# Attention passes of a graph network: the weights of a group move from SBUF into PSUM, behind the scan's multipliers

## The chip, the cores and the metric

One Trainium2 chip, one of its cores. The metric is the device time of one execution in microseconds. The kernel before was run three times: median 13124.66 us, 13120.15 to 13129.22 us.

## What is computed

Four graph layers follow one another over 12500 nodes and 200000 edges sorted by target node, each behind a layer norm and added to its input. The change touches the attention of the second and third layer. For every edge a score is made per head, a softmax runs over the edges of one target node, and the weighted rows of the source nodes are summed:

```python
e = alpha_s[src] + alpha_d[dst]
e = jnp.where(e > 0, e, NEG_SLOPE * e)
m = jax.ops.segment_max(e, dst, num_segments=num_nodes)
w = jnp.exp(e - m[dst])
denom = jax.ops.segment_sum(w, dst, num_segments=num_nodes)
alpha = w / (denom[dst] + 1e-16)
out = jax.ops.segment_sum(alpha[:, :, None] * h[src], dst, num_segments=num_nodes)
```

This attention runs three times with 4 heads of 16 features: once in the second layer (there the score has an edge term too) and twice in the third.

## The kernel before

Each of the 128 partitions owns 1563 consecutive edges. A pass (`gat_edges`, L2070) walks over them in 98 groups of 16 edge columns; the last two groups are cut into four smaller pieces. The rows of the source nodes land in a ring `y` of six groups (an iteration of the loops is these six). Of the 96 columns of an iteration three sources fetch:

- GpSimd (POOL) gathers 86 by indirect DMA, one instruction a column (L2129; 1403 in a pass). It waits only for the ring's slot to be free, by the signal `weighted` (L2126).
- SyncE (SP) fetches two, row by row with 128 small DMAs each (`SyncRows`, L338; its DMAs are L333), after the same signal.
- TensorE fetches eight out of a table in SBUF by matmuls with a unit matrix (`ColumnFetch`, L382; the matmuls are L475). VectorE adds up what they give (L483) and picks the half that is wanted (L511, L514); these are the "points" in VectorE's step.

VectorE then does one `step` for each group: scores (L2195 to L2204), running maximum by scans (L2210), differences (L2222 to L2226), then, once ScalarE has written the weights `ex` = exp(s - max) (L2285): a copy of `ex` into the scan's input (L2232), the weighting of the rows, a multiply of 1024 elements a partition, `y` by `ex` into `w_in` (L2233, which raises `weighted`), and the scan that carries the softmax sum along the edges with the multipliers `r` = exp(old max - new max) (L2240, which raises `summed`). ScalarE's part of a group, in its order: exp for `ex`, exp for `r` (L2290, 1088 elements), the load of the next edge attributes (L2305, second layer's pass alone), the load of TensorE's places (L451, L456), and the finished rows `row` out to memory (L2298 to L2302). The `r` lies in three banks of PSUM of which it uses 1156 of 1536 words; `ex` lies in SBUF.

The order around the change is set by each engine's own program order and by these semaphores:

```python
act.wait_ge(*shifted(pc.n + 1))
...
act.activation(ex[:, :, 0:w], de[:, 1, :, 0:w], ACT.Exp).then_inc(exps.h, 1)
act.wait_ge(*summed(pc.n))
...
v.wait_ge(*weighted[b](i + 1))
v.wait_ge(*r_ready(g + 1))
```

`summed(pc.n)` is the scan of the group before, which VectorE has done before it raises `shifted`. The passes of the first layer (`conv_edges`, L1012) are built alike, with one head of 97 features; their gathers are L1059, their weighting is L1118 (1552 elements), and their `ex` lies in PSUM, in a bank of its own.

Of the kernel before, what the change touches and what calls it, by code (L numbers as in the profile page):

```python
# [25 lines left out]
P = 128  # L26
# [4 lines left out]
GW = 16  # L31
# [74 lines left out]
def piece(i, b):  # L106

    return Piece(i * 2 + b, i, b, b, i, 0, GW, (i * 2 + b) * GW, GW)
# [51 lines left out]
def narrow(t, w):  # L160

    flat = t.rearrange("p f t -> p (f t)")
    return flat[:, 0:flat.shape[1] // (GW + 1) * (w + 1)].rearrange("p (f t) -> p f t", t=w + 1)
# [90 lines left out]
def build(nc, a, out):  # L254
# [13 lines left out]
    h = table[:, NCOL // 2:].rearrange("p (c f) -> p c f", f=D)  # L268
# [37 lines left out]
    def by_edge(t):  # L306
        return t[0:EP, :].rearrange("(p t) f -> p t f", p=P)
# [1762 lines left out]
    def gat_edges(tag, rows, bd=None):  # L2070

        H, J1 = HG, JG + 1
        F = H * J1
        st = Stage(nc, tag, signals)
        y = st.sb("y", [P, NY, GW, TG])
        ad_raw, ad = st.sb("ad_raw", [P, ET, H]), st.sb("ad", [P, H, ET])
        s0, s, fm = st.sb("s0", [P, H, GW]), st.sb("s", [P, H, GW]), st.sb("fm", [P, 2, H, GW + 1])
        de, ex, ex_bank = st.sb("de", [P, 2, H, GW]), st.sb("ex", [P, H, GW]), st.ps("z0", [P, 512])
        r_banks, w_in = st.ps("r", [P, 1536]), st.sb("w_in", [P, H, J1, GW + 1])
        r_flat = r_banks[:, 0:F * (GW + 1)].rearrange("p (f t) -> p f t", f=F)  # L2080
        r, w_flat = (r_banks[:, 0:F * (GW + 1)].rearrange("p (h j t) -> p h j t", h=H, j=J1),
# [15 lines left out]
            eadded = st.sem("eadded", NPIECE)  # L2097
        taken = SYNC_SLOTS + [c.slot for c in FETCHED]
        gathered, by_sync = st.pass_slots(taken), SyncRows(st, y, g_tab, TG, 1)
        other_bank = [] if bd is not None else [st.ps("z1", [P, 512])[:, 0:2 * TG]]  # L2100
        fetch = ColumnFetch(st, (pa, pb), [ex_bank[:, 0:2 * TG]] + other_bank,
                            row[:].rearrange("p b t f -> p (b t f)")[:, 0:1024].rearrange("p (b f) -> p b f", b=2),
# [3 lines left out]
        weighted, row_ready, den_in = (st.piece_slots(n) for n in ("weighted", "row_ready", "den_in"))  # L2106
# [3 lines left out]
        exps, r_ready, summed = (st.sem(n, NPIECE) for n in ("exps", "r_ready", "summed"))  # L2110
# [3 lines left out]
        with nc.Block(no_gpsimd_drain=True) as block:  # L2114
            @block.sync
            def _(sp):
                sp.wait_ge(*signals["scattered0"](0))
                sp.dma_start(ad_raw[:], by_edge(ad_start)).then_inc(ad_loaded.h, 16)
                by_sync.all_columns(sp, weighted)
# [156 lines left out]
            @block.scalar  # L2276
            def _(act):
                def weights(pc):
                    w = pc.w
                    act.wait_ge(*shifted(pc.n + 1))  # L2280
                    if pc.b == 1:
                        act.wait_ge(*weighted[0](pc.i + 1))
                    else:
                        act.wait_ge(*weighted[1](pc.i))
                    act.activation(ex[:, :, 0:w], de[:, 1, :, 0:w], ACT.Exp).then_inc(exps.h, 1)  # L2285
                    act.wait_ge(*summed(pc.n))
                    if w < GW:
                        act.activation(narrow(r_flat, w)[:, :, 0:1], same[:, 0:1].unsqueeze(1).to_broadcast([P, F, 1]),
                                       ACT.Copy, scale=0.0)
                    act.activation(narrow(r_flat, w).rearrange("p (h j) t -> p h j t", h=H)[:, :, :, 1:w + 1],  # L2290
                                   de[:, 0, :, 0:w].unsqueeze(2).to_broadcast([P, H, J1, w]), ACT.Exp)\
                        .then_inc(r_ready.h, 1)

                def send(pc):
                    b, w = pc.b, pc.w
                    act.wait_ge(*summed(pc.n + 1))
                    act.wait_ge(*row_stored[b](pc.i * 16))
                    act.activation(row[:, b, 0:w, F:F + H], fm[:, b, :, 1:w + 1].rearrange("p h t -> p t h"), ACT.Copy)  # L2298
                    act.activation(row[:, b, 0:w, 0:F], narrow(acc[:, b], w)[:, :, 1:w + 1].rearrange("p f t -> p t f"),  # L2299
                                   ACT.Copy).then_inc(row_ready[b].h, 1)  # L2300
                    act.wait_ge(*row_ready[b](pc.i + 1))
                    act.dma_start(by_edge(rows)[:, bass.ds(pc.col, w), :], row[:, b, 0:w]).then_inc(row_stored[b].h, 16)  # L2302

                def edge_attrs(i, b, w=GW):
                    act.dma_start(ea[0:8 * w, b, :], a["edge_attr_8"][bass.ds((i * 2 + b) * P, 8 * w), :])\  # L2305
                        .then_inc(e_loaded[b].h, 16)

                def group(n, j, more=True):
                    i, b = n * (NY // 2) + j // 2, j % 2
                    weights(piece(i, b))  # L2310
                    if bd is not None:
                        act.wait_ge(*e_scored[b](i + 1))
                        edge_attrs(i + 1, b, GW if more or j < NY - 1 else GL)
                    if j == 1 and more:
                        fetch.load_early(act, n + 1)
                    send(piece(i, b))
                    if j == 4 and more:
                        fetch.load_late(act, n + 1)

                fetch.load_early(act, 0)  # L2320
                fetch.load_late(act, 0)
                act.dma_start(wgx[:], wg_d).then_inc(wg_loaded.h, 16)
                fetch.load_masks(act)
                if bd is not None:
                    for b in range(2):
                        edge_attrs(0, b)
                act.activation(same_ps[0], same[:, 0:cut], ACT.Copy).then_inc(same_copied.h, 1)
                act.activation(same_ps[1], same[:, cut:ET], ACT.Copy).then_inc(same_copied.h, 1)
                fetch.high_thirds(act)
                with act.Fori(0, NITER - 1) as n:  # L2330
                    for j in range(NY):
                        group(n, j)
                for j in range(NY):
                    group(NITER - 1, j, False)
                for pc in LASTS:
                    weights(pc)
                    send(pc)
                fix_on_scalar(act)
# [675 lines left out]
    with ExitStack() as gat:  # L3014
        bd = gat.enter_context(nc.sbuf_tensor("bd", [P, HG * GW], F32))
        conv_to_gat("n2", rows_d[1], a["L0_gnn_v2_w"], a["L0_gnn_v2_b"], a["L0_gnn_e2_w"], a["L0_gnn_s2_w"],
                    a["L0_gnn_s2_b"], a["L0_gnn_skip_w"], a["L0_gnn_skip_b"], a["gat_w"],
                    a["L1_gnn_a_s"].rearrange("h o -> (h o)"), a["L1_gnn_a_t"].rearrange("h o -> (h o)"), HG,
                    (bd, a["gat_we"], a["L1_gnn_a_e"].rearrange("h o -> (h o)")))
        block_diagonal("bd", bd)  # L3020
        gat_edges("c3", rows_d[2], bd)
        gat_to_gat("n3", rows_d[2], a["L1_gnn_b_GAT"].rearrange("h o -> (h o)"), False, a["L2_gnn_W1"],
                   a["L2_gnn_a_src1"].rearrange("h o -> (h o)"), a["L2_gnn_a_dst1"].rearrange("h o -> (h o)"), HG)
        gat_edges("c4", rows_d[3])
        gat_to_gat("n4", rows_d[3], a["L2_gnn_b1"], True, a["L2_gnn_W2"],
                   a["L2_gnn_a_src2"].rearrange("h o -> (h o)"), a["L2_gnn_a_dst2"].rearrange("h o -> (h o)"), 1)
        gat_edges("c5", rows_d[4])
        gat_to_pna("n5", rows_d[4], a["L2_gnn_b2"])
# [43 lines left out]
```

## Time and profile before

| | |
|---|---|
| median of the runs | 13124.66 us |
| profiled execution, its own time | 13120.87 us |
| its span | 13119.1 us |
| POOL busy | 9811.0 us (75%) |
| DVE busy | 7263.4 us (55%) |
| ACT busy | 4121.0 us (31%) |
| PE busy | 2341.8 us (18%) |
| granted TensorE clock, mean | 0.595 of full |

Busy time counts an engine's own instructions. The three attention passes lie between 4687 and 10814 us of the span. A share over the whole span says little about them; the rows further down are taken from these stretches.

### The profile page before, as it was taken

Reading aid. Unit: us, or ns where it says so; the run is one execution under the profiler, and the core shown is the slowest. Engines: PE = TensorE matmul, PEld = TensorE weight load, DVE = VectorE, ACT = ScalarE, POOL = GpSimd, SP = SyncE. Lnnn points to the kernel's source line nnn. Section 1 sums busy time; section 2 is a strip of 40 time slices with the busy share of each in tenths; the row PEclk is TensorE's granted clock in tenths of the full one; section 3 lists DMA queues with packets and bytes.
Section 4 is the critical chain, followed back from the end, with each engine's and each line's share of the span. In section 5 each row is a group of like instructions: output and inputs, shape, how many; then the busy total and the mean of one; then the engine's idle time right before and its main releaser. Section 6 shows DMA issues by size and latency. Waiting matters only on the chain. (4 is left out here: it accounts for less than half of the span.)

```text
span 13119.1 us, 196710 instructions
## 1 busy us (share of the span) xinstructions
PE 2341.8 (18%) x51836; PEld 1979.8 (15%) x51836; DVE 7263.4 (55%) x11947; ACT 4121.0 (31%) x4096; POOL 9811.0 (75%) x10026
## 2 busy tenths in 40 slices
PE   3000001200000243333223333313333320000001
PEld 1000000100000133333213222212332220000000
DVE  2777776377777544444434444444444446556656
ACT  4333333233333322121212111112111113666663
POOL 7777776777777677777777777777777776777775
PEclk9999999555555655555555555555555555555555
DMA  8445444344444222222212222222222223444443
GB/s 337 121 124 129 123 124 106 88 124 124 120 123 122 74 60 68 65 66 64 64 41 67 61 61 63 61 58 58 62 62 61 61 60 106 158 159 157 162 161 117
DMA packets 957876, 1318.90 MB, mean 101 GB/s; under 512 B 643852, under 2 KB 661427, under 8 KB 943088
## 3 DMA queue, kind: packets, MB, share of 16 engines
q10 hardware_dynamic: 547843, 802.76, 19.0%
q0 software_dynamic: 323648, 361.44, 14.2%
q1 hardware_dynamic: 85292, 141.67, 3.0%
q8 instruction: 500, 8.19, 0.3%
q14 instruction: 593, 4.85, 0.1%
HBM read 645.09 MB, written 659.95 MB: 99 GB/s over the span
## 5 line engine op out<-in xcount | busy, mean ns | idle before, releaser
L2129 POOL DMA_INDIRECT c_y<-g_tab,srcs x4209 | 4299.4, 1021 | 1284.1 <-issue 1284.1
L2624 POOL DMA_INDIRECT c_y<-h_tab,srcs x1547 | 1460.4, 944 | 506.4 <-issue 471.4
L1059 POOL DMA_INDIRECT c_y<-h_tab,srcs x1531 | 1444.7, 944 | 466.9 <-issue 466.9
L1059 POOL DMA_INDIRECT first_y<-h_tab,srcs x1452 | 1370.2, 944 | 444.9 <-issue 442.3
L2195 DVE TENSOR_TENSOR c_s<-c_y,c_ad 128x64 f32<-128x64 f32 x300 | 79.5, 265 | 2213.8 <-DMA c_y<-g_tab,srcs 2213.8
L475 PE MATMUL c_pb<-table,unit 128*128 x24576 | 764.2, 167 | 1607.6 <-issue 1607.6
L475 PE MATMUL c_pa<-table,unit 128*128 x24576 | 764.0, 167 | 1367.5 <-issue 1367.5
L475 PEld LDWEIGHTS c_pb<-table,unit 128*128 128x128 bf16 x24576 | 719.9, 103 | 1690.9 <-issue 1690.9
L475 PEld LDWEIGHTS c_pa<-table,unit 128*128 128x128 bf16 x24576 | 719.8, 103 | 1456.6 <-issue 1456.6
L2285 ACT ACTIVATE c_ex<-c_de 128x64 f32<-128x64 f32 x300 | 76.5, 255 | 2582.5 <-DVE c_de L2226 2582.1
L2240 DVE TENSOR_TENSOR_SCAN c_acc<-c_r,c_w_in 128x1156 f32<-128x1156 f32 x300 | 753.9, 2513 | 10.3
L1081 DVE TENSOR_TENSOR_SCAN c_q_all<-c_mask,c_q_in 128x408 f32<-128x408 f32 (+2 forms) x800 | 734.5, 986 | 16.4 <-issue 9.0
L1125 DVE TENSOR_TENSOR_SCAN c_acc<-c_r,c_w_in 128x408 f32<-128x408 f32 (+2 forms) x800 | 732.2, 978 | 6.9
L1267 PE MATMUL c_q_all<-ident,carry_v 128*97 128x128 f32 x2 | 1.1, 531 | 3940.7 <-DVE c_mrep L1281 3940.7
L1174 ACT ACTIVATE c_q_in<-c_q_raw 128x1552 f32<-128x1552 f32 (+1 forms) x200 | 596.9, 2984 | 267.8 <-DVE c_q_in L1141 197.8
L2299 ACT ACTIVATE c_row<-c_acc 128x1088 f32<-128x1088 f32 x300 | 618.3, 2061 | 0.0
L1188 ACT ACTIVATE c_ex<-c_de 128x16 f32<-128x16 f32 (+1 forms) x200 | 37.4, 187 | 1779.1 <-DVE c_de L1114 1779.1
L1267 PEld LDWEIGHTS c_q_all<-ident,carry_v 128*97 128x97 f32 x2 | 0.5, 236 | 3941.5 <-DVE c_mrep L1281 3941.5
L2233 DVE TENSOR_TENSOR c_w_in<-c_y,c_ex 128x1024 f32<-128x1024 f32 x300 | 585.5, 1952 | 0.0
L1202 ACT ACTIVATE c_row<-c_acc 128x1552 f32<-128x1552 f32 (+1 forms) x200 | 565.0, 2825 | 0.0
L2668 DVE TENSOR_TENSOR_SCAN c_acc_s<-c_mask,c_su 128x442 f32<-128x442 f32 (+4 forms) x500 | 478.3, 1024 | 133.4 <-ACT c_su L2761 133.2
L2298 ACT ACTIVATE c_row<-c_fm 128x64 f32<-128x64 f32 x300 | 92.5, 308 | 1457.0 <-DVE c_acc L2240 1457.0
(447 smaller groups left out, 9224.6 us busy)
## 6 DMA issues: line engine op xcount, KB each, us to landing
c_y<-g_tab SPq DMA_DIRECT2D x12288, 0.3 KB
rows_d<-c_row ACTq DMA_DIRECT2D x96, 2048.0 KB
rows_d<-c_row ACTq DMA_DIRECT2D x288, 576.0 KB
c_q_raw<-q_start ACTq DMA_DIRECT2D x194, 776.0 KB, 6.1
rows_d<-c_row ACTq DMA_DIRECT2D x192, 784.0 KB
c_y<-h_tab SPq DMA_DIRECT2D x6144, 0.2 KB
q_start<-first_y SPq DMA_DIRECT2D x97, 776.0 KB, 8.8
c_y<-g_tab,srcs POOLq DMA_INDIRECT x4209
```

The lines of the kernel that those rows point to most:

```text
L475: last = nc.tensor.matmul(self.f_ps[f % 2][:, 3 * k:3 * k + 3], unit[:], third_bytes[:, :, bass.ds(spot, 2)].bitcast(BF16).rearrange("p s ...
L1059: nc.gpsimd.indirect_dma_start(y[:, g % NY, k, 0:D], None, h_tab, source(g, k))\
L1081: last = v.tensor_tensor_scan(flat(qs[:, lo:hi]), flat(mk[:, 0:hi - lo]), flat(q_cur[:, lo:hi]), 0.0, ALU.mult, ALU.add)
L1125: last = v.tensor_tensor_scan(flat(ac[:, lo:hi]), flat(rr[:, 0:hi - lo]), flat(w_cur[:, lo:hi]), 0.0, ALU.mult, ALU.add)
L1174: act.activation(narrow(q_in[:, pc.b], pc.w)[:, :, 1:pc.w + 1], q_raw[:, pc.slot, pc.lo:pc.lo + pc.w].rearrange("p t f -> p f t"), ACT.Copy)
L1202: act.activation(row[:, b, 0:w, 0:F], narrow(acc[:, b], w)[:, :, 1:w + 1].rearrange("p f t -> p t f"), ACT.Copy).then_inc(row_ready[b].h, 1)
L2129: nc.gpsimd.indirect_dma_start(y[:, g % NY, k, :], None, g_tab, source(g, k))\
L2233: v.tensor_tensor(w_heads[:, :, 0:JG, 1:w + 1], ys[:, :, 0:D].rearrange("p t (h j) -> p h j t", h=H), ex[:, :, 0:w].unsqueeze(2).to_broadc ...
L2240: v.tensor_tensor_scan(flat(ac), flat(rr), flat(w_cur), 0.0, ALU.mult, ALU.add).then_inc(summed.h, 1)
L2299: act.activation(row[:, b, 0:w, 0:F], narrow(acc[:, b], w)[:, :, 1:w + 1].rearrange("p f t -> p t f"), ACT.Copy).then_inc(row_ready[b].h, 1)
L2624: nc.gpsimd.indirect_dma_start(y[:, g % NY, k, :], None, h_tab, source(g, k))\
L2668: last = v.tensor_tensor_scan(flat(ac_s[:, lo:hi]), flat(mk[:, 0:hi - lo]), flat(su_c[:, lo:hi]), 0.0, ALU.mult, ALU.add)
```

## The change

The tile `ex` is dropped from SBUF. Its 64 words a partition now lie at the end of the three PSUM banks of `r` (words 1472 to 1535; `r` ends at 1156), so in the third bank both stand together. ScalarE writes `ex` as before. Before it writes `r` it no longer waits for the scan of the group before, but for the weighting of this group, so that `r` is not written while VectorE reads `ex`. No instruction is added or taken away, and no engine's order changes.

```diff
-        de, ex, ex_bank = st.sb("de", [P, 2, H, GW]), st.sb("ex", [P, H, GW]), st.ps("z0", [P, 512])
+        de, ex_bank = st.sb("de", [P, 2, H, GW]), st.ps("z0", [P, 512])
...
+        ex = r_banks[:, 1536 - H * GW:1536].rearrange("p (h t) -> p h t", h=H)
...
                     act.activation(ex[:, :, 0:w], de[:, 1, :, 0:w], ACT.Exp).then_inc(exps.h, 1)
-                    act.wait_ge(*summed(pc.n))
+                    act.wait_ge(*weighted[pc.b](pc.i + 1))
```

## Rows read from the trace of the kernel before

**Rows 1.** Groups on POOL: name, count | busy us, mean ns | idle before, releaser.

```profile
L2129 POOL DMA_INDIRECT c_y<-g_tab,srcs x4209 | 4299.4, 1021 | 1284.1 <-issue 1284.1
...
L1059 POOL DMA_INDIRECT c_y<-h_tab,srcs x1531 | 1444.7, 944 | 466.9 <-issue 466.9
```

**Rows 2.** Timeline of one group: start us, length us, engine, line.

```profile
5513.40 1.06 ACT L2290 ACTIVATE c_r<-c_de 128x1088 f32<-128x1088 f32 x1
...
5514.62 1.99 DVE L2233 TENSOR_TENSOR c_w_in<-c_y,c_ex 128x1024 f32<-128x1024 f32 x1
5515.48 1.88 POOL L2129 DMA_INDIRECT c_y<-g_tab,srcs  x1 [0.30 <-issue]
...
5516.64 2.56 DVE L2240 TENSOR_TENSOR_SCAN c_acc<-c_r,c_w_in 128x1156 f32<-128x1156 f32 x1
5517.67 0.95 POOL L2129 DMA_INDIRECT c_y<-g_tab,srcs  x1 [0.30 <-issue]
```

**Rows 3.** Two weightings by line: count, ns min/median/max, first and last start, forms.

```profile
L2233 DVE TENSOR_TENSOR c_w_in<-c_y,c_ex x300: 362/1994/2025, 4769.8 to 10812.4; 128x1024 f32<-128x1024 f32 x144, 128x512 f32<-128x512 f32 x6
...
L1118 DVE TENSOR_TENSOR c_w_in<-c_y,c_ex x100: 487/2983/3058, 2514.7 to 4414.2; 128x1552 f32<-128x1552 f32 x96, 128x776 f32<-128x776 f32 x3, 128x291 f32<-128x291 f32 x1
```

**Rows 4.** Timeline, VectorE: end of the first pass, and the last scan of each.

```profile
6513.82 0.27 DVE L2195 TENSOR_TENSOR c_s<-c_y,c_ad 128x64 f32<-128x64 f32 x1 [9.56 <-DMA c_y<-g_tab,srcs]
...
6520.98 0.23 DVE L2243 COPY c_w_in<-c_acc 128x68 f32<-128x68 f32 x1
6524.31 0.21 DVE L2195 TENSOR_TENSOR c_s<-c_y,c_ad 128x32 f32<-128x32 f32 x1 [3.10 <-DMA c_y<-g_tab,srcs]
...
6529.14 0.23 DVE L2243 COPY c_w_in<-c_acc 128x68 f32<-128x68 f32 x1
...
6553.14 0.72 DVE L2240 TENSOR_TENSOR_SCAN c_acc<-c_r,c_w_in 128x272 f32<-128x272 f32 x1
...
8679.13 0.72 DVE L2240 TENSOR_TENSOR_SCAN c_acc<-c_r,c_w_in 128x272 f32<-128x272 f32 x1
...
10812.78 0.72 DVE L2240 TENSOR_TENSOR_SCAN c_acc<-c_r,c_w_in 128x272 f32<-128x272 f32 x1
```

**Rows 5.** Timeline, VectorE's points L483 while it runs behind POOL, first pass.

```profile
4841.70 0.56 DVE L483 TENSOR_REDUCE c_fx<-c_pa 128x128 f32<-128x384 f32 x1 [5.69 <-PE c_pa L475]
...
4905.12 0.56 DVE L483 TENSOR_REDUCE c_fx<-c_pb 128x128 f32<-128x384 f32 x1 [2.44 <-PE c_pb L475]
...
4942.17 0.56 DVE L483 TENSOR_REDUCE c_fx<-c_pa 128x128 f32<-128x384 f32 x1 [5.60 <-PE c_pa L475]
```

**Rows 6.** Timeline, POOL: first gather of each of the three passes.

```profile
4687.66 0.96 POOL L2129 DMA_INDIRECT c_y<-g_tab,srcs  x1 [0.30 <-issue]
...
6816.62 1.07 POOL L2129 DMA_INDIRECT c_y<-g_tab,srcs  x1 [0.30 <-issue]
...
8943.11 1.06 POOL L2129 DMA_INDIRECT c_y<-g_tab,srcs  x1 [0.30 <-issue]
```

**Rows 7.** Timeline, SP's queue: starts of columns, some cut short by the window asked.

```profile
4699.17 48.84 SPq L333 DMA_DIRECT2D c_y<-g_tab  x128
...
5507.49 49.41 SPq L333 DMA_DIRECT2D c_y<-g_tab  x128
...
5562.89 6.68 SPq L333 DMA_DIRECT2D c_y<-g_tab  x21
...
6829.31 1.61 SPq L333 DMA_DIRECT2D c_y<-g_tab  x5
...
7797.82 49.53 SPq L333 DMA_DIRECT2D c_y<-g_tab  x128
...
8955.78 1.29 SPq L333 DMA_DIRECT2D c_y<-g_tab  x4
...
9814.25 1.85 SPq L333 DMA_DIRECT2D c_y<-g_tab  x6
```

## The prediction

> **What bounds the kernel now.** I read the groups of POOL first, because POOL is the busiest engine, then the timeline of one group, then the ends of the passes. In the three attention passes POOL issues 4209 gathers, and in front of every one of them it sits idle for 1284.1 / 4209 = 0.305 us with nothing to wait for [rows 1]. So its queue runs without a stop, and VectorE, which waits 9.56 us for the gathered rows of group 95 [rows 4], follows it. A pass lasts as long as POOL's 1403 gathers. One gather takes 1.021 us in the mean here, but 0.944 us in the first layer's pass [rows 1]. With 0.944 us for all, the 4209 would need 3973.3 us in place of 4299.4: **326.1 us** are lost, 109 us a pass, 1.11 us a group.
>
> Where they are lost stands in the timeline [rows 2]. A gather that starts at 5515.48, during the weighting (5514.62 to 5516.61), lasts 1.88 us and ends at 5517.36, 0.75 us after the weighting. The next one starts at 5517.67, inside the scan (5516.64 to 5519.20), and lasts 0.95 us. The weighting reads two operands from SBUF, the rows and `ex`. The scan reads one from SBUF and one from PSUM. The same contrast stands between passes: the first layer's weighting takes `ex` from PSUM, lasts 2.98 us a group [rows 3], and its gathers are at 0.944 us [rows 1]. So I read: a gather that starts during a long VectorE instruction with two SBUF operands is held until that ends, and one PSUM operand sets it free.
>
> The Trainium skill, "SBUF — State Buffer", section "Who interferes with whom", says that a VectorE instruction with two SBUF inputs contends with a GpSimd instruction that reads SBUF; the rows above agree. The same section notes that a multiply of two tensors did not stall the generation of DMA descriptors; by that remark the held gathers would not be the weighting's doing and the change would free nothing, which is the second rival. The held gather at 5515.48 speaks against that.
>
> **The change part by part.**
>
> *`ex` in PSUM.* One group's weighting no longer holds a gather: -1.11 us on POOL for each of 98 groups, -109 us a pass, if POOL stays the bound. The weighting itself, with a PSUM operand, is in no row of these passes. The nearest is the first layer's, 2983 ns for 1552 elements, 1.92 ns each, so 1.97 us for 1024; today it takes 1.994 [rows 3]. Bounds: 2.27 us by the scan's 2.56 us for 1156 [rows 2], and below 1.0 us, about the pace of ScalarE's 1.06 us for 1088. I take 2.0, no change. The copy of 64 words at L2232 may gain or lose up to 0.2 us, as long as a whole copy of 68 words takes (0.23) [rows 4]; I take nothing.
>
> *The new wait.* Today `r` is written at 5513.40 to 5514.46, ahead of the weighting, in its shade [rows 2]. Now it follows the weighting, and the scan follows `r`: 1.06 us and two handoffs between engines, which I bound from 0 to 0.5 each and take as 0.07. So VectorE's step of a whole group grows from 7.39 us (6513.82 to 6521.21) to 8.6, and of a half one from 5.06 to about 5.8 [rows 4]. Cover: POOL's group, 1403 x (0.944 + 0.305) / 98 = 17.9 us against today's 19.0, leaves VectorE's wait of 9.56 us some 7 us long. Without that cover the 1.2 us would cost 1.2 x 300 = 360 us and eat the gain. `weighted`, which POOL and SP wait for, is raised by the weighting itself and is not late. Queued behind the wait on ScalarE are the edge attributes' load, TensorE's places and the rows out, later by up to 2.0 + 1.2 us; all are for groups two or more ahead.
>
> *TensorE's columns.* Where VectorE runs behind POOL, at the start of the first pass, an iteration of six groups takes 4942.17 - 4841.70 = 100.5 us, and VectorE waits for TensorE at its points, 2.44 to 5.69 us [rows 5]. A step that is 1.2 us later stays within the least of these. The new iteration on POOL is 86 x 1.249 = 107.4 us (today 86 x 1.326 = 114.1), so TensorE's 100.5 still fits.
>
> *SP, next in line.* SP runs ahead in each pass's first half, unhindered, and shows its own pace: 8 pairs of columns in 5562.89 - 4699.17 us, 107.97 us a pair; 9 pairs, 107.61 us, in the second pass; 8 pairs, 107.31 us, in the third [rows 7]. Against POOL's 107.4 this is a tie, and SP begins 12 us later. So SP's last column will end after POOL's work for the same group, and **this decides the end of a pass**. The pause after a pair is 5562.89 - 5507.49 - 49.41 = 6.0 us. The 16th pair ends at 4699.17 + 16 x 107.97 - 6.0 = 6420.7, 8545.1 and 10666.8. From there: landing (an estimate, 0 to 4 us, taken 2), step of group 95 (8.6), three half pieces (17.4), the last piece (4, estimated as less than a half): 32 us. Ends by SP: 6452.7, 8577.1, 10698.8. Ends by POOL (first gather [rows 6] + 1403 x 1.249 = 1752.3, + landing and the last piece, 6): 6446.0, 8574.9, 10701.4. The later of each against today's 6553.86, 8679.85 and 10813.50 [rows 4] gives -101.2, -102.8 and -112.1: **-316 us**. Nothing outside these passes changes.
>
> The profiled execution took 13120.87 us, 3.8 less than the median of the runs shown. 13120.87 - 316 = **12805 us**. The limits of this case: all 326 us and 10 us of spread below, 12785. Above, what the tie can cost if SP, TensorE and VectorE get in each other's way: up to the SP's lag again, some 20 us a pass, 12870.
>
> **The rivals.**
>
> *A. TensorE's chain pays the wait.* Each of the eight columns of an iteration passes through VectorE's point; if each point comes 1.2 us late for TensorE, an iteration takes 100.5 + 9.6 = 110.1 us. Gain then (114.1 - 110.1) x 16.3 x 3 = 196 us: 12925. For it: TensorE runs only two columns ahead. Against it: the waits of rows 5, all on VectorE's side. Chance 0.08.
>
> *B. The gathers stay held,* by the result's write or by the other small instructions with two SBUF operands, whatever `ex` does. Then POOL's stream is unchanged, and the ends of the passes pay the four last pieces' added waits, some 4 us each: +12, 13133. For it: the skill's remark. Against it: the scan and the first layer's weighting write as much and hold nothing. Chance 0.04.
>
> *C. Slower.* The mechanism is A with ScalarE's queue added: a point is late by the 1.2 us, and TensorE's loads and attributes by the 2.0 us of weighting ahead of them, 3.2 us for each column. An iteration then takes 100.5 + 8 x 3.2 = 126.1 us, 12.0 more than POOL's today: +12.0 x 16.3 x 3 = 587, 13708. It decides from (114.1 - 100.5) / 8 = 1.7 us a column on. Against it: the loads serve columns of the next iteration, and POOL's margin of a whole ring. Chance 0.03.
>
> **How the numbers follow.** The forecast has 0.85, with 12785 to 12870; that alone holds the 8 in 10 wanted. About 0.2%, 26 us, is what a measurement of this kernel can tell from no change. Faster: the forecast and A, 0.93. Same: B, 0.04. Slower: C, 0.03.
>
> **What would show it.** Right: POOL's gathers of these passes at a mean below 0.95 us with at most some 20 us lost in all; `r` written after each weighting and the scan about 1.2 us behind it; in each pass's second half SP's pauses at 2.9 and 5.5 us, as in the first, and VectorE waiting at groups 2 and 5 of an iteration for SP's rows. POOL's gathers would still follow without a wait. Wrong: gathers of 1.9 us beside the weighting (B); TensorE's fetches 110 us an iteration or more with waits for VectorE (A, C); or the weighting at another length than 2.0 us, which would move only the ends.

## The result and the profile after

The changed kernel takes **12813.81 us** in the median of three runs (12806.26 to 12814.86) against 13124.66 us before: a ratio of 0.9761, 95% interval 0.9739 to 0.9784. The forecast was 12805 us, 9 us below.

| | before | after |
|---|---|---|
| profiled execution, its own time | 13120.87 us | 12813.81 us |
| its span | 13119.1 us | 12812.0 us |
| POOL busy | 9811.0 us | 9498.6 us |
| DVE busy | 7263.4 us | 7261.4 us |
| ACT busy | 4121.0 us | 4144.9 us |
| PE busy | 2341.8 us | 2339.6 us |

The POOL groups of the page (name, count | busy us, mean ns | idle before, releaser) answer to [rows 1]; the changed file has one line more, so L2129 is now L2130:

```profile
L2130 POOL DMA_INDIRECT c_y<-g_tab,srcs x4209 | 3980.2, 946 | 1283.6 <-issue 1283.6
...
L1059 POOL DMA_INDIRECT c_y<-h_tab,srcs x1531 | 1446.8, 945 | 467.0 <-issue 467.0
```

The same 4209 gathers take 3980.2 us in place of 4299.4, as long each as those of the first layer. This row gains 319.2 us and POOL's sum 312.4 (9811.0 - 9498.6): its other groups together took 6.8 us longer. VectorE's sum has hardly moved (-2.0 us).

The timeline of one group (start us, length us, engine, line; [wait before, releaser]) answers to [rows 2]:

```profile
5528.71 0.94 POOL L2130 DMA_INDIRECT c_y<-g_tab,srcs  x1 [0.31 <-issue]
...
5529.09 1.97 DVE L2234 TENSOR_TENSOR c_w_in<-c_y,c_r 128x1024 f32<-128x1024 f32 x1
5529.96 0.94 POOL L2130 DMA_INDIRECT c_y<-g_tab,srcs  x1 [0.31 <-issue]
5531.10 1.08 ACT L2291 ACTIVATE c_r<-c_de 128x1088 f32<-128x1088 f32 x1 [9.61 <-DVE c_w_in L2234]
5531.21 0.95 POOL L2130 DMA_INDIRECT c_y<-g_tab,srcs  x1 [0.30 <-issue]
...
5532.27 2.56 DVE L2241 TENSOR_TENSOR_SCAN c_acc<-c_r,c_w_in 128x1156 f32<-128x1156 f32 x1 [1.21 <-issue]
```

A gather that starts at 5529.96, in the middle of the weighting (5529.09 to 5531.06), lasts 0.94 us; in [rows 2] its like lasted 1.88. Counted over the trace before, 97 or 98 gathers of a pass last over 1.2 us; after, none does. In each of the 288 whole groups before, exactly one gather that starts in the weighting is held, and it ends 0.76 to 0.78 us behind the weighting. After, 454 gathers start in a weighting, and the longest of them lasts 0.95 us. (The weighting's operand reads `c_r`, since `ex` lies in those banks.) ScalarE now writes `r` behind the weighting, 0.04 us after its end, and the scan starts 0.09 us after `r`: 1.21 us of idle VectorE.

What VectorE waits for (us in total, times, longest us):

```profile
DVE c_s L2196 <- DMA c_y<-g_tab: 913.9, 79, 19.0
DVE c_s L2196 <- DMA c_y<-g_tab,srcs: 637.2, 126, 10.1
```

The second row is POOL's gathers, the first SP's fetches. Before, 2213.8 us stood on POOL's gathers alone. So the waits are shorter, and the larger part of them is now for SP.

Last, the end of the second pass on VectorE, which answers to [rows 4], and the last pair of columns on SP's queue (start, length), which answers to [rows 7]:

```profile
8449.01 0.27 DVE L2196 TENSOR_TENSOR c_s<-c_y,c_ad 128x64 f32<-128x64 f32 x1 [18.99 <-DMA c_y<-g_tab]
8451.29 1.98 DVE L2234 TENSOR_TENSOR c_w_in<-c_y,c_r 128x1024 f32<-128x1024 f32 x1
8454.48 2.57 DVE L2241 TENSOR_TENSOR_SCAN c_acc<-c_r,c_w_in 128x1156 f32<-128x1156 f32 x1 [1.21 <-issue]
8457.08 0.43 DVE L2244 COPY c_w_in<-c_acc 128x68 f32<-128x68 f32 x1
...
8463.79 0.23 DVE L2244 COPY c_w_in<-c_acc 128x68 f32<-128x68 f32 x1
...
8469.50 0.23 DVE L2244 COPY c_w_in<-c_acc 128x68 f32<-128x68 f32 x1
...
8475.20 0.23 DVE L2244 COPY c_w_in<-c_acc 128x68 f32<-128x68 f32 x1
...
8478.26 0.72 DVE L2241 TENSOR_TENSOR_SCAN c_acc<-c_r,c_w_in 128x272 f32<-128x272 f32 x1 [0.61 <-DVE c_w_in L2234]
```

```profile
8344.88 102.80 SPq L333 DMA_DIRECT2D c_y<-g_tab  x256
```

SP's last column ends at 8344.88 + 102.80 = 8447.68. Group 95 starts 1.33 us later, after a wait of 18.99 us for it, and from there VectorE runs to the last scan at 8478.98 without another wait for rows. So SP set the end of this pass.

Measured from a pass's first gather to the end of its last scan (read off the trace for each pass, as in [rows 4, 6]):

| pass | before, us | after, us | saved |
|---|---|---|---|
| 1 | 1866.2 | 1762.1 | 104.1 |
| 2 | 1863.2 | 1763.4 | 99.8 |
| 3 | 1870.4 | 1761.7 | 108.7 |
| the rest of the span | 7519.3 | 7524.9 | -5.6 |

The rest is 5.6 us longer: 2.8 ahead of the first of these passes, 2.5 behind the last.

### The profile page after: what moved, and what is told of

Same layout as the page of the kernel before. It is cut to its first block and busy times, and to the rows that moved or that the text cites. A ratio compares the mean times of both kernels' runs of the same rounds, so it can differ in the third digit from the quotient of the medians.

```text
span 12812.0 us, 196575 instructions
## 1 busy us (share of the span) xinstructions
PE 2339.6 (18%) x51836; PEld 1977.5 (15%) x51836; DVE 7261.4 (57%) x11947; ACT 4144.9 (32%) x4096; POOL 9498.6 (74%) x10026
## 5 line engine op out<-in xcount | busy, mean ns | idle before, releaser
L2130 POOL DMA_INDIRECT c_y<-g_tab,srcs x4209 | 3980.2, 946 | 1283.6 <-issue 1283.6
L2625 POOL DMA_INDIRECT c_y<-h_tab,srcs x1547 | 1462.0, 945 | 506.0 <-issue 471.3
L1059 POOL DMA_INDIRECT c_y<-h_tab,srcs x1531 | 1446.8, 945 | 467.0 <-issue 467.0
L1059 POOL DMA_INDIRECT first_y<-h_tab,srcs x1452 | 1372.0, 945 | 444.9 <-issue 442.3
L2196 DVE TENSOR_TENSOR c_s<-c_y,c_ad 128x64 f32<-128x64 f32 x300 | 79.2, 264 | 1551.3 <-DMA c_y<-g_tab 913.9
L2286 ACT ACTIVATE c_r<-c_de 128x64 f32<-128x64 f32 x300 | 67.9, 226 | 1992.7 <-DVE c_de L2227 1940.2
L2291 ACT ACTIVATE c_r<-c_de 128x1088 f32<-128x1088 f32 x300 | 317.9, 1060 | 1090.2 <-DVE c_w_in L2234 1061.6
L2234 DVE TENSOR_TENSOR c_w_in<-c_y,c_r 128x1024 f32<-128x1024 f32 x300 | 582.9, 1943 | 0.0
```

Of the source, the lines that this page charges most:

```text
L1059: nc.gpsimd.indirect_dma_start(y[:, g % NY, k, 0:D], None, h_tab, source(g, k))\
L2130: nc.gpsimd.indirect_dma_start(y[:, g % NY, k, :], None, g_tab, source(g, k))\
L2234: v.tensor_tensor(w_heads[:, :, 0:JG, 1:w + 1], ys[:, :, 0:D].rearrange("p t (h j) -> p h j t", h=H), ex[:, :, 0:w].unsqueeze(2).to_broadc ...
L2625: nc.gpsimd.indirect_dma_start(y[:, g % NY, k, :], None, h_tab, source(g, k))\
```

## The experiments

The theory: a gather that starts during a long VectorE instruction with two SBUF operands is held until that instruction ends; one operand in PSUM sets it free. The rivals: `r`'s later writing frees it (the change has two parts), the copy of `ex` holds as well, or it isn't the operands' place at all. "Before" in each paragraph is the kernel before on the same chip.

### The new wait alone

The kernel before, `ex` in SBUF, with the change's wait:

```diff
-                    act.wait_ge(*summed(pc.n))
+                    act.wait_ge(*weighted[pc.b](pc.i + 1))
```

> The kernel before with the new wait alone: the weights stay in SBUF, the multipliers are written after the weighting. Theory (the weighting holds gathers because both its operands lie in SBUF): gathers of the three passes stay at a mean of about 1.02 us, some 320 us lost in all; the ends of the passes pay three half pieces and the last one, 0.9 us each, or about 4 us a pass: 13125 + 12, about 13135. Rival (it was the writing of the multipliers beside the weighting that held the gathers, and the wait cured it): a mean near 0.946 us and about 12815.

It took 13114.05 us against 13121.17, one run each. Its timeline:

```profile
5505.09 1.99 DVE L2233 TENSOR_TENSOR c_w_in<-c_y,c_ex 128x1024 f32<-128x1024 f32 x1
5505.29 2.56 POOL L2129 DMA_INDIRECT c_y<-g_tab,srcs  x1 [0.30 <-issue]
5507.11 1.08 ACT L2290 ACTIVATE c_r<-c_de 128x1088 f32<-128x1088 f32 x1 [3.80 <-DVE c_w_in L2233]
...
5508.28 2.57 DVE L2240 TENSOR_TENSOR_SCAN c_acc<-c_r,c_w_in 128x1156 f32<-128x1156 f32 x1 [1.20 <-issue]
```

The gather is held to 5507.85, 0.77 us behind the weighting, though `r` is now late. The wait frees nothing. Nor does it cost much: a pass's last scan ends 7.1 to 7.4 us behind its last gather, against 5.7 to 5.9 before, so about 1.5 us a pass. The passes are no longer than before (5594.3 us in sum against 5599.8), so the 12 us expected do not show in the time; POOL lost 316 us here and 326 before.

### Which reader of `ex`: the weighting or the copy

Two variants of the changed kernel. ScalarE writes `ex` twice, into SBUF and into PSUM, and one of the two readers takes the SBUF one: the weighting (first variant) or the copy of 64 words ahead of it (second).

```diff
+        ex_sb = st.sb("ex", [P, H, GW])
...
+                    act.activation(ex_sb[:, :, 0:w], de[:, 1, :, 0:w], ACT.Exp)
...
-                                    ex[:, :, 0:w].unsqueeze(2).to_broadcast([P, H, JG, w]), ALU.mult)\
+                                    ex_sb[:, :, 0:w].unsqueeze(2).to_broadcast([P, H, JG, w]), ALU.mult)\
```

```diff
-                    v.tensor_copy(w_heads[:, :, JG, 1:w + 1], ex[:, :, 0:w]).then_inc(den_in[b].h, 1)
+                    v.tensor_copy(w_heads[:, :, JG, 1:w + 1], ex_sb[:, :, 0:w]).then_inc(den_in[b].h, 1)
```

> The changed kernel, but ScalarE writes the weights twice, to PSUM and to SBUF; the copy of 64 words reads PSUM, the weighting reads SBUF again. Theory: held as before, mean about 1.02 us, about 13140 (13125 + 12, and a second exp of 0.23 us in each step). Rival (the copy from SBUF to SBUF was what held the gathers): mean near 0.946 us, about 12820.

> The mirror of the last: weights written twice, the copy reads SBUF, the weighting reads PSUM. Theory: free, mean near 0.946 us, about 12818 (12814 and some us for the second exp at the ends). Rival (the copy holds them): mean about 1.02 us, about 13140.

They took 13117.94 and 12810.37 us against 13121.17, one run each. The gathers of the first, then of the second:

```profile
L2131 POOL DMA_INDIRECT c_y<-g_tab,srcs x4209 | 4289.2, 1019 | 1283.8 <-issue 1283.8
```

```profile
L2131 POOL DMA_INDIRECT c_y<-g_tab,srcs x4209 | 3975.4, 944 | 1284.1 <-issue 1284.1
```

With nothing but the weighting's operand back in SBUF the whole gain is gone; with nothing but the copy's operand there, none of it is. The weighting's operand is the cause.

### Another instruction made to hold

The changed kernel with the scan's multipliers `r` moved into SBUF. Now the weighting has one operand in PSUM and the scan, 2.57 us, has two in SBUF.

```diff
+        r_sb = st.sb("r_sb", [P, F * (GW + 1)])
...
-        r, w_flat = (r_banks[:, 0:F * (GW + 1)].rearrange("p (h j t) -> p h j t", h=H, j=J1),
+        r, w_flat = (r_sb[:].rearrange("p (h j t) -> p h j t", h=H, j=J1),
```

> The changed kernel, but the scan's multipliers lie in SBUF, so the scan (2.56 us) has two SBUF operands and the weighting one. Theory: any long VectorE instruction with two SBUF operands holds the gather that starts in it until 0.75 us after its end. A gather starts every 1.25 us, so the first one starts on the mean 0.62 us into the instruction and would have taken 0.944: the loss is length - 0.62 + 0.75 - 0.944 = length - 0.82. For the weighting's 1.99 us that is 1.17 (measured before: 1.11). For the scan 1.74 us, 98 x 3 x 1.74 = 512 us: about 13325, mean of a gather about 1.067 us. Rival (something about the weighting's own access, its stride or its repeated operand, held them): mean near 0.946 us, about 12815.

It took 13302.02 us in one run, 181 more than before. The gathers' group, and a timeline:

```profile
L2131 POOL DMA_INDIRECT c_y<-g_tab,srcs x4209 | 4474.6, 1063 | 1283.7 <-issue 1283.7
```

```profile
6005.63 1.99 DVE L2235 TENSOR_TENSOR c_w_in<-c_y,c_r 128x1024 f32<-128x1024 f32 x1
6005.95 0.94 POOL L2131 DMA_INDIRECT c_y<-g_tab,srcs  x1 [0.31 <-issue]
...
6008.85 2.57 DVE L2242 TENSOR_TENSOR_SCAN c_acc<-c_r_sb,c_w_in 128x1156 f32<-128x1156 f32 x1 [1.24 <-issue]
6009.70 2.47 POOL L2131 DMA_INDIRECT c_y<-g_tab,srcs  x1 [0.30 <-issue]
```

Now the gather in the weighting is free (0.94 us) and the one in the scan is held to 6012.17, 0.75 us behind the scan's end. Over 0.944 us each, 501 us are lost, where the kernel before lost 326. So, for the multiply as for the scan, the place of the operands decides, and the instruction's length sets the price.

### One long instruction or two short ones

The kernel before, `ex` in SBUF, the weighting written as two instructions of two heads each:

```diff
+                    for h0 in (0, 2):
+                        half = v.tensor_tensor(w_heads[:, h0:h0 + 2, 0:JG, 1:w + 1], rows_h[:, h0:h0 + 2],
...
+                    half.then_inc(weighted[b].h, 1)
```

> The kernel before (weights in SBUF, multipliers early) with the weighting cut into two instructions of 512 elements, about 1.07 us each, one behind the other. If a held gather gets through between the two (held by one instruction alone), it ends 0.75 us after the first half: the loss per half is at most 1.07 + 0.75 - 0.944 = 0.88 us, on the mean over where a gather starts in 1.25 us 0.88 x 0.88 / 2 / 1.25 = 0.31, for two halves 0.6 us a group: some 180 us in all in place of 326, about 12975. If the second half takes the port again before the gather is done, the loss stays near 1.1 us a group, about 13121.

It took 12944.48 us against 13128.4, one run each. Its group and its timeline:

```profile
L2129 POOL DMA_INDIRECT c_y<-g_tab,srcs x4209 | 4123.2, 980 | 1283.8 <-issue 1283.2
```

```profile
5519.44 2.07 DVE L2235 TENSOR_TENSOR c_w_in<-c_y,c_ex 128x512 f32<-128x512 f32 x2
5520.18 1.11 POOL L2129 DMA_INDIRECT c_y<-g_tab,srcs  x1 [0.30 <-issue]
...
5521.60 0.94 POOL L2129 DMA_INDIRECT c_y<-g_tab,srcs  x1 [0.30 <-issue]
```

The two halves take 2.07 us together, so the first ends at about 5520.48 and the second at 5521.51. The gather ends at 5521.29, 0.8 us behind the first and before the second is done; the next one starts when both are over. Here a gather is held by one instruction, not by a stretch of such work. The loss falls from 326 to 150 us without any operand leaving SBUF, 30 us below the 180 that were expected.

### What bounds the changed kernel

Is it still POOL, or has SP become as slow? The changed kernel with four of POOL's 86 gathers of an iteration left out (their columns hold zeros):

```diff
+LEFT_OUT = [2, 3, 4, 5]
...
+    kept += [0] if g % NY in LEFT_OUT else []
...
-        taken = SYNC_SLOTS + [c.slot for c in FETCHED]
+        taken = SYNC_SLOTS + [c.slot for c in FETCHED] + LEFT_OUT
```

> The changed kernel with 4 of POOL's 86 gathers in each iteration left out (column 0 of ring slots 2 to 5 holds zeros instead of rows). POOL then needs 82 x 1.25 = 102.5 us an iteration. Theory (SP, at 107.6 us a pair of columns, was next in line): the passes still last until SP's last column and 32 us, 1758 to 1762 us; the time falls by 0 to 15 us, 12800 to 12814. Rival (POOL alone bounds the passes): 64 gathers a pass x 1.25 x 3 = 240 us less, about 12575.

And then SP's load cut as well, 96 of 128 rows singly and the other 32 in one DMA (other rows than those wanted):

```diff
+        by_sync = SyncRows(st, y, g_tab, TG, 1, rows=3 * P // 4)
...
-            for lo in range(0, P, NREG):
+            for lo in range(0, self.rows, NREG):
...
+                sp.dma_start(self.y[self.rows:P, SYNC_SLOTS[b], SYNC_K, 0:self.width], self.tab[self.rows:P, :])\
```

> As the last, and of each SP column only 96 rows are fetched one by one, the other 32 by one DMA of rows that stand together (wrong rows): a pair of columns takes SP about 2 x 37.4 + 8.4 = 83 us. Theory: POOL is the bound again at 102.5 us an iteration, and TensorE's 100.5 us fits below it without paying the new wait: passes of about 1339 x 1.25 + 7 = 1681 us, 81 less each, about 12572. Rival A (TensorE's columns pay the 1.2 us of the wait, up to 110 us an iteration): no less than 12800; in between, TensorE pays a part.

The first took 12810.59 us (two runs), ratio to before 0.9759 [0.9739, 0.9779]: nothing gained over the change. VectorE's wait for SP's rows:

```profile
DVE c_s L2198 <- DMA c_y<-g_tab: 1212.2, 79, 24.8
```

It has grown from 913.9 to 1212.2 us, the view lists no wait of this line for POOL's gathers any more, and a pass's last scan ends 77 to 81 us behind POOL's last gather. The second took 12557.41 us, ratio 0.9566 [0.9547, 0.9585], and there VectorE waits for POOL again:

```profile
DVE c_s L2202 <- DMA c_y<-g_tab,srcs: 1040.8, 178, 10.3
```

Its passes last 1680 us, 1339 gathers x 1.249 and 7. So in the changed kernel POOL and SP end a pass nearly together, and lightening POOL alone brings nothing. SP alone was not lightened. By the traces it could bring little: the change's passes end 7.3 to 9.0 us behind POOL's last gather, and where POOL alone set the end, with the wait alone, it was 7.1 to 7.4, so some 2 us a pass at most (an estimate). TensorE's eight columns, the bound of rival A, keep pace with an iteration of 82 x 1.249 = 102.4 us.

### `ex` in a bank of its own

In the third layer's two passes a PSUM bank is free. There `ex` can have it, `r` can be written early again, and the wait falls away:

```diff
+        own = r_banks[:, 1536 - H * GW:1536] if bd is not None else st.ps("ex", [P, 512])[:, 0:H * GW]
...
-                    act.wait_ge(*weighted[pc.b](pc.i + 1))
+                    act.wait_ge(*(weighted[pc.b](pc.i + 1) if bd is not None else summed(pc.n)))
```

> The changed kernel, but in the second and third pass, which have a PSUM bank to spare, the weights lie in that bank and the multipliers are written before the weighting again, as in the kernel before. Theory (the new wait of 1.2 us a step is hidden but at the ends): those two passes end up to 3.2 and 1.4 us earlier (they end 9.0 and 7.3 us behind the last gather, before the change 5.9), 12809 to 12814; gathers unchanged at 0.946 us. Rival (VectorE's step is on the path): 1.2 us for each of 200 groups, 240 us, about 12575.

It took 12794.78 us (12789.45 to 12803.01), ratio 0.9748 [0.9732, 0.9764], 19 us less than the change had shown, which is more than expected. To see how much of that was the chip, the change and this kernel ran once more, side by side, five rounds:

> The changed kernel once more, as the measure for the next one on the same chip: about 12810 to 12815; passes of 1762 us each, 5287 us together.

> The kernel with a bank of its own for the weights in the second and third pass, once more. If the shorter steps at the ends of these two passes are all it gains: about 9 us below the changed kernel on the same chip (its passes lasted 5277.7 us together, those of the changed kernel 5287.2). If that difference was one of two chips: no difference.

The change took 12820.24 us (12819.49 to 12826.61), ratio 0.9755 [0.9742, 0.9769]; the own bank 12815.39 us (12814.90 to 12819.38), ratio 0.9751 [0.9738, 0.9764]; before was at 13141.18 there. The third pass's end, POOL's last gather and the last scan, with the change and then with the own bank:

```profile
10500.06 0.94 POOL L2130 DMA_INDIRECT c_y<-g_tab,srcs  x1 [0.30 <-issue]
...
10507.65 0.72 DVE L2241 TENSOR_TENSOR_SCAN c_acc<-c_r,c_w_in 128x272 f32<-128x272 f32 x1 [0.61 <-DVE c_w_in L2234]
```

```profile
10497.26 0.95 POOL L2131 DMA_INDIRECT c_y<-g_tab,srcs  x1 [0.30 <-issue]
...
10503.00 0.72 DVE L2242 TENSOR_TENSOR_SCAN c_acc<-c_r,c_w_in 128x272 f32<-128x272 f32 x1
```

The last scan ends 7.4 us behind the last gather, and 5.5 with the own bank: the wait costs 1.9 us at this end, 1.5 at the second pass's. The two passes together are 3.9 us shorter, and the medians are 4.9 apart, about half of the 9 expected. The two ratios' intervals overlap almost wholly, so against before the two can't be told apart; side by side, each of the own bank's five runs lies below each of the change's five, if only by 0.1 us at the closest. Against the first runs both kernels are slower here, the change by 6.4 us and the own bank by 20.6, so most of the 19 us lay between sets of runs. In the own bank's two traces the difference stands in POOL's gathers: those of the attention passes take 3985.8 us in place of 3975.8, and the three groups of the other layers' gathers (from `h_tab`) 4285.7 in place of 4275.3, each gather 2 to 3 ns longer. Why, no run shows.

## Why the prediction was right

It was right in mechanism, sign and size; the sum was 316 us and the profiled execution is 307.1 us shorter. By its own steps:

***`ex` in PSUM.*** 1.11 us a group were to come back on POOL. They did: over 0.944 us a gather, 2.2 to 2.4 us are lost in a pass after, 105 to 113 before. Two experiments pin it to the weighting's operand, and a third makes the scan hold in its stead. The weighting was taken at 2.0 us with a PSUM operand and takes 1.98, so the operand's place cost VectorE nothing. The Trainium skill, "SBUF — State Buffer", section "Who interferes with whom", says that a VectorE instruction with two SBUF inputs contends with a GpSimd instruction that reads SBUF, not with one that only writes it; POOL's gather, whose indices `srcs` lie in SBUF, behaves so in all of these runs. The same section's remark that `tensor_tensor`, which the multiply is, did not stall DMA does not hold for this gather: 1019 ns with the multiply's operands in SBUF, 946 with one in PSUM. That was rival B, and it fell.

***The new wait.*** Group 95's step was to grow from 7.39 to 8.6 us. It measures 8.57 in the first pass, 8.50 in the second (8449.01 to 8457.51) and 8.35 in the third. Exp was taken as 1.06 us and the handoffs as 0.07 each, 1.2 together; they take 1.08, 0.04 and 0.09, 1.21 together. A half piece was to take 5.8: from one copy's end to the next, the second and third of the second pass take 5.71 and 5.70, the first 6.51. The cover held: through the passes the waits for rows took up the 1.2 us. It shows at the ends alone.

***TensorE's columns.*** An iteration of 107.4 us was to fit over TensorE's 100.5. It did, and with POOL and SP lightened 102.4 us fitted too. That is below rival A's 110.1 us an iteration and rival C's 126.1, so neither came about. Where VectorE runs behind POOL, at the start of the first pass, VectorE's points answer to [rows 5]:

```profile
4841.17 0.56 DVE L483 TENSOR_REDUCE c_fx<-c_pa 128x128 f32<-128x384 f32 x1 [3.67 <-PE c_pa L475]
...
4880.97 0.56 DVE L483 TENSOR_REDUCE c_fx<-c_pb 128x128 f32<-128x384 f32 x1 [1.08 <-PE c_pb L475]
...
4939.03 0.56 DVE L483 TENSOR_REDUCE c_fx<-c_pa 128x128 f32<-128x384 f32 x1 [3.61 <-PE c_pa L475]
```

The least wait is 1.08 us where it was 2.44: the later step came out of VectorE's waits here, as was argued. The iteration takes 4939.03 - 4841.17 = 97.9 us, less than the 100.5 before, which was not foreseen. With the wait alone it takes 97.5 to 98.2, counted from scan to scan, so the shortening comes with the wait; why, no run shows.

***SP, next in line.*** SP was to end its last column 1733.0, 1728.5 and 1723.7 us after the passes' first gathers; it did so after 1726.7, 1732.1 and 1730.4. Each is off by 4 to 7 us, in both directions. The pace was read from one stretch of each pass of the kernel before, eight or nine pairs with the first among them; in the changed kernel pairs follow one another after 107.5 to 109.7 us in all three passes, but the first and the last after 104.0 to 105.4. The signs that the step named were there: in the second half of each pass SP pauses 2.9 us within a pair and 5.4 to 5.8 after it, as in the first (but for the last pair), and all of VectorE's 79 waits for SP's rows stand at groups 2 and 5 of an iteration. From that column to the last scan 32 us were taken. Where SP alone sets the end it is 31.3 (second pass) and 31.2 (third), with landings (from the end of SP's column to VectorE's first use) of 1.0 to 1.3 us where 2 were taken. In the first pass it is 35.4, because the last half piece waits 3.50 us for POOL's gather. There SP was 6.3 us earlier than forecast and the way from it 3.4 us longer; that the two errors partly cancel is luck. So the step named the wrong engine twice, for the first pass (SP alone, where POOL came in too) and for the third (POOL by 2.6 us, where SP was last). In a tie that close the engine could not be told, and the time hardly depended on it: 101.2, 102.8 and 112.1 us were forecast and 104.1, 99.8 and 108.7 measured, 3.5 us less in sum.

***Nothing else changes.*** The rest of the span was 5.6 us longer, which no part of the change touches. The three groups of the other layers' gathers (from `h_tab`, L1059 twice and L2625) took 1.6, 2.1 and 1.8 us longer, about 1 ns a gather, so nearly all of it is POOL's pace in that run. With the 3.5 us that makes up the 9 us between forecast and profile. The repeats of the change lie between 12806 and 12827 us over two sets of runs, so these 9 us are no finding.

**Rival B's price.** It put the added wait at a pass's end at some 4 us, as four pieces' waits. The wait alone shows 1.5 us, and the own bank gives back 1.5 to 1.9. Only the last pieces come behind POOL's last gather; for the others the wait lies beside gathers still to come.

## What to carry to other kernels

Where GpSimd's gathers are the bound, look for gathers that last longer than the rest and for the VectorE instruction that they overlap: if that reads two SBUF operands and is long, move its smaller operand into PSUM, and if there is no room, cut it into shorter instructions (here that alone took the loss from 326 to 150 us). The operand may even share a bank that another engine writes, at the price of a wait, as long as VectorE has slack through the loop; the wait is then paid once at the end of each pass, here 1.5 to 1.9 us. Before speeding up one of several engines that feed the same loop, work out the pace of the next one from a stretch where it runs unhindered, since that sets what can be gained.

## What the runs showed of the hardware that was not expected

The price of a long instruction follows its length. A held gather ends 0.75 to 0.78 us behind the instruction, and a free gather takes 0.944. If it starts at a random point of POOL's cycle of 1.249 us, so 0.62 us into the instruction in the mean, an instruction longer than that cycle, of length L, costs L - 0.62 + 0.75 - 0.944 = L - 0.81 us (an estimate from these rows). For the weighting of 1.99 us that gives 1.18; measured was 326 / 294 = 1.11. For the scan of 2.57 us it gives 1.76; measured was 501 / 294 = 1.70.

Halving the instruction saved more than half of the loss, 176 of 326 us, where the length rule, extended to the halves, gave less. In the group shown, the gather that the first half held lasted nearly to the second's end, and the next one met neither. Counted over the trace, that is so in 211 of the 288 whole groups; in 67 the second half holds a gather, and in 10 neither does.

Short instructions with two SBUF operands hold next to nothing: the scores' adds of 0.2 to 0.3 us remain in the changed kernel, and its gathers lose 2.2 to 2.4 us in a pass of 1403, no more a gather than those of the first layer in the same run. The same rule gives why (an estimate): a gather that starts with an instruction of 0.27 us and ends 0.75 us behind it lasts 1.02 us, 0.08 more than a free one, and one that starts in its last 0.19 us loses nothing.
